# A four-stage transformer kernel on eight cores: a different spread of background quantize jobs in the MLP stage, and a layer norm whose row sums come from two half-row copies

## What is computed

```python
# layer 0, "attention": linear attention and an inner MLP
a = _ln(num / den, ga, ba)
h = a + (gelu(a @ W1 + b1) @ W2 + b2)          # W1 1024x4096, W2 4096x1024
x = _layernorm(x + (h + x))
# layer 0, feed-forward: FP4 block quantization of activations and weights
x = _layernorm(x + fp4_linear(silu(fp4_linear(x, w_gate)) * fp4_linear(x, w_up), w_down))
# layer 1, causal softmax attention, then a squared-relu feed-forward
x = _layernorm(x + attention(x))
x = _layernorm(x + ffn(x))

def fp4_quant_dequant(x):      # blocks of 16 along the last dim
    scale = max(|xb|) / 6
    q = GRID[searchsorted(MID, |xb / scale|)] * sign(xb) * scale
```

## Time and profile before

| what | us |
|---|---|
| median of the two runs | 6672.61 |
| the two runs | 6623.13 and 6722.09 |
| time of the profiled execution | 6682.19 |
| its span (slowest core, core 3) | 6679.5 |
| spans of the eight cores | 6587.1 to 6679.5 |
| DVE busy in the span | 3081.2 (46%) |
| PE busy in the span | 3082.8 (46%) |
| ACT busy in the span | 1331.5 (20%) |
| MLP of phase 1, from the first job at its head to the last job after it | 1613 to 3025 |

### The profile page before, as it was taken

The page is one execution under the profiler, slowest core; times in us unless marked ns, Lnnn a source line. Parts: engine busy times, 40 slices in busy tenths (PEclk is TensorE's granted clock), DMA queues, the critical chain, the costliest instruction groups (busy, mean ns, idle before and its releaser), DMA issues.

```text
span 6679.5 us, 50329 instructions; the slowest of 8 cores (6587.1 to 6679.5 us)
## 1 busy us (share of the span) xinstructions
PE 3082.8 (46%) x11857; PEld 1206.4 (18%) x11857; DVE 3081.2 (46%) x6040; ACT 1331.5 (20%) x2575; POOL 166.1 (2%) x315
## 2 busy tenths in 40 slices
PE   5436154000515243430355555542876666667553
PEld 2112012000202021210123222211321111112321
DVE  4453635642262625348782838473433333333442
ACT  3213110300101011110112111112023333333223
POOL 0000000011000000000000000000000000000000
PEclk8657565555757676665577777776865555557676
DMA  3111010037221212120000000000200000000201
GB/s 49 32 29 21 29 24 14 25 60 158 72 71 60 83 55 89 38 95 5 19 1 29 1 29 1 20 0 21 43 13 1 0 0 0 0 0 24 40 1 51
DMA packets 101208, 217.43 MB, mean 33 GB/s; under 512 B 13506, under 2 KB 17858, under 8 KB 99906
## 3 DMA queue, kind: packets, MB, share of 16 engines
q0 software_dynamic: 39008, 102.27, 7.2%
q1 hardware_dynamic: 61922, 111.96, 5.0%
HBM read 226.26 MB, written 38.27 MB: 40 GB/s over the span
## 4 chain that ended last, share of the span: by engine, by line
DVE 36%; PE 31%; issue 13%; DMA 9%; ACT 8%; DVEq 2%; POOL 1%; SPq 1%; ACTq 0%; POOLq 0%
PE ps L350 17%; DVE QSC L921 8%; PE ps L1127 4%; PE ps L1106 3%; DVE xstage L1138 3%; PE ps L804 2%; DVE QG L872 2%; PE psb L383 2%; ACT ROT L1113 2%; DVE QSC L895 2%; DVE QSC L897 2%; ACT DUM L847 1%; DVE QSC L912 1%; DVE QSC L914 1%; DVE QSC L923 1%
## 5 line engine op out<-in xcount | busy, mean ns | idle before, releaser
L350 PE MATMUL ps<-G 128*128 128x512 f16 (+1 forms) x3328 | 816.1, 409 | 1057.4 <-ACT G L785 600.8
L350 PEld LDWEIGHTS ps<-G 128*128 128x128 f16 x3328 | 362.8, 111 | 1486.0 <-issue 1251.2
L921 DVE TENSOR_TENSOR QSC<-QSC 128x1024 f16<-128x1024 f16 (+2 forms) x888 | 544.1, 613 | 93.4 <-DVE QSC L895 0.9
L350 PE MATMUL ps<-WAbB,G 128*128 128x512 f16 x1536 | 411.1, 429 | 211.0 <-DMA BR<-bq_row 115.2
L1113 ACT ACTIVATE ROT<-ps 128x512 f16<-128x512 f32 x640 | 375.2, 597 | 635.3 <-DVE G L1148 305.7
L1127 PE MATMUL ps<-ROT,GV 128*65 128x512 f16 x640 | 398.3, 622 | 154.4 <-DVE ROT L1120 110.0
L804 PE MATMUL ps<-WAbB,G 128*128 128x512 f16 x1024 | 299.5, 463 | 263.8 <-DMA WAbB<-w2scr 195.0
L888 ACT ACTIVATE xstage<-xstage 128x1024 f32<-128x1024 f32 (+1 forms) x68 | 70.1, 1031 | 1540.5 <-DVE bct L881 892.6
L1106 PE MATMUL ps<-G 64*128 64x512 f16 x640 | 374.7, 606 | 0.0
L383 PE MATMUL psb<-identb_s,G 128*128 128x128 f16 x640 | 82.1, 304 | 597.6 <-DVE G L394 446.9
L1120 DVE TENSOR_TENSOR ROT<-ROT,trimask_s 128x128 f16<-128x128 f16 x256 | 57.7, 226 | 490.0 <-ACT ROT L1113 469.3
(11 more groups left out here) (189 smaller groups left out, 4049.2 us busy)
## 6 DMA issues: line engine op xcount, KB each, us to landing
WAbB<-w2scr SPq DMA_DIRECT2D x256, 256.0 KB, 4.7
xstage<-w_gate POOLq DMA_DIRECT2D x22, 512.0 KB, 4.4
xstage<-w_up POOLq DMA_DIRECT2D x22, 512.0 KB, 4.4
WAbB<-wgoA SPq DMA_DIRECT2D x44, 256.0 KB, 4.0
ROT<-x POOLq DMA_DIRECT2D x32, 256.0 KB, 4.0
WAbB<-W POOLq DMA_DIRECT2D x32, 256.0 KB, 8.9
w2scr<-WAbB SPq DMA_DIRECT2D x32, 256.0 KB, 8.7
xstage<-w_down POOLq DMA_DIRECT2D x16, 512.0 KB, 4.4
```

Source lines behind the costliest of these rows:

```text
L350: last = h.matmul(psbanks[i], lhs_list[j], rhs_list[j][i], start=(j == 0), stop=(j == nchain - 1 and not extra))
L921: lambda h: h.tensor_tensor(Q, Q, C, op=ALU.add))
```

## The change

Two edits. In the MLP of phase 1 the drain at the head of a chunk takes six jobs where it took four, and the two drains after the half-chunks take two where they took three. The number of jobs in a chunk stays ten, and their order is the same.

In `ln_plain_tile` the in-place 1024-wide Copy becomes two 512-wide Copies into `DUM`, so there are four ACT instructions of one size. `ln_stats_math` loses its `full_sum` form: the two sums are added first (one more tiny DVE instruction). The tile is no longer written back by ACT.

```diff
-        def ln_stats_math(slot, full_sum=False):
+        def ln_stats_math(slot):
-            if full_sum:
-                p.op("vector", [sk(0)], [sk(4)],
-                     lambda h, b0=b0: h.tensor_scalar(STAT[:, b0 + 4:b0 + 5],
-                                                      STAT[:, b0:b0 + 1],
-                                                      1.0 / D, None, op0=ALU.mult))
-            else:
...
+            p.op("vector", [sk(0), sk(1)], [sk(4)],
+                 lambda h, b0=b0: h.tensor_tensor(STAT[:, b0 + 4:b0 + 5], STAT[:, b0:b0 + 1],
+                                                  STAT[:, b0 + 1:b0 + 2], op=ALU.add))
+            p.op("vector", [sk(4)], [sk(4)],
+                 lambda h, b0=b0: h.tensor_scalar(STAT[:, b0 + 4:b0 + 5], STAT[:, b0 + 4:b0 + 5],
+                                                  1.0 / D, None, op0=ALU.mult))
...
             for tc in range(TC):
-                bg_drain(4)
+                bg_drain(6)
...
                         ln_plain_tile(ROT, sl, R, tt)
-                    bg_drain(3)
+                    bg_drain(2)
...
-            p.op("scalar", [src.k(sblk)], [src.k(sblk), sk(0)],
-                 lambda h, b0=b0: h.activation(src.blk(sblk), src.blk(sblk), AF.Copy,
-                                               accum_out=STAT[:, b0:b0 + 1]))
-            for i_, c0 in ((2, 0), (3, 512)):
+            for i_, (c0, func) in enumerate(((0, AF.Copy), (512, AF.Copy),
+                                             (0, AF.Square), (512, AF.Square))):
                 p.op("scalar", [src.k(sblk)], [sk(i_), "DUMk"],
-                     lambda h, c0=c0, i_=i_, b0=b0: h.activation(
-                         DUM[:, :], src.blk(sblk, c0, c0 + 512), AF.Square,
+                     lambda h, c0=c0, func=func, i_=i_, b0=b0: h.activation(
+                         DUM[:, :], src.blk(sblk, c0, c0 + 512), func,
                          accum_out=STAT[:, b0 + i_:b0 + i_ + 1]))
-            mAP, rAP, mk_, rk_ = ln_stats_math(slot, full_sum=True)
+            mAP, rAP, mk_, rk_ = ln_stats_math(slot)
```

## The result

The changed kernel is slower by 1.48%: ratio 1.0148, 95% interval 1.0093 to 1.0203, which just leaves open whether it is over 2%. Its median is 6780.15 us (11 runs), that of the kernel before 6718.3 (10 runs). The profiled execution took 6720.52 us, with a span of 6717.9.

The account below looks back on a forecast made before the run. The prediction took hand-overs to bound the kernel, chiefly PE idle 600.8 us before Gelus held behind quantize jobs. Jobs 94.0, earlier adds -9.3 and norm +21.3 gave +106.0 on 6682.19: 6788 us, range 6735 to 6835 (forecast's own 6745 to 6825).

Parts of the forecast that it names:

- The jobs' term: Phase 1's MLP: four full-width quantize jobs move from PE's cover to the path, 23.5 us each, +94.0 us.
- the narrow ones cancel: Covered jobs in phase 1's MLP: narrow jobs 52 and 64 before, 55 and 64 after, so four full-width jobs move.
- The give-back: Second half-chunks of phase 1's MLP: shorter cover lets the residual add start earlier, by 2.7, 5.8, 0.8 and 0: -9.3 us.
- The norm's term: Layer norm: ACT's fourth instruction adds 0.38 us a tile, exposed in 56 of 64 tiles, +21.3 us.
- The test I had named for this term: Norm term is wrong if DVE's last-Square wait stays at 1.48 us a tile while tiles keep their pace.
- The half-spread of 50 us: Whole kernel: the two runs shown lie 99 us apart, so a run can miss the sum by some 50 us.
- The free norm: Rival, layer norm: ACT's extra instruction costs 0 to 0.09 us on the path, 6767 to 6772 us; chance 0.08.
- the uncovered third job: Rival, MLP half-chunks: third job was never covered, so shedding it repays the head, 6703.5 us; chance 0.05.
- this rival: Rival, MLP up stages: three lose clock to the last one's rate, 3 x 10.5 = 31 us, 6820 us; chance 0.12.
- Cheaper jobs at the head: Rival, first head of the MLP: longer run hides loads, 17.9 us a job, 6766 us; chance 0.03.

## Why the prediction was right

**The mechanism.** Each step of the argument from the earlier trace rows is in the changed profile: the absolute value ahead of the Gelus, the eight jobs in a row, the 20 us of idle DVE under the half-chunk (20.71), the stand of 178 us (forecast near 180), the sum of 709.8 (near 710).

**The jobs' term, +94.0.** The first head grew by 47.1 us and the end shrank by 23.6, as two periods and one. That the 47.1 is so near is in part luck, since the head starts up to 28 us apart on the four cores; but from the first job of the head to the first Gelu it is 75.7 to 77.4 us on the eight cores before and 122.1 to 123.4 after, two periods of 23.2. The three runs grew by 56.7. Counting their jobs one by one gives 23.5 (a full one more), 20 (the added one is narrow) and 24, since of a run's last job only the part up to its absolute value counts. That is 67.5, and the prediction had 70.5: "the narrow ones cancel" was 3 us off.

**The give-back, -9.3.** This term was sized on one core, and it differs from core to core: over the four chunks the second half-chunk's add had started later than the 0.2 us behind PE by 12.7, 12.5, 13.7 and 7.9 us in sum on cores 4 to 7, all with a clock of 0.653 or 0.654. On core 6 it was 4.9, 3.7, 3.4 and 1.7 us. After the change it is 0.2 us behind PE's end in every chunk on every core, as predicted. With the median of the first three chunks on die 1, 11.1, the runs come to 67.5 - 11.1 + 6 x 0.38 = 58.7, against 56.7 measured.

**The norm's term, +21.3.** 3.33 us a tile, to the hundredth; 5.6 and 5.8 us in the two stretches of 15 tiles, where 5.7 was expected; phase 4's tail 5.1. The estimate worked out from the figures of the Trainium skill's page "ScalarE: Activation LUTs", section "What ACT_TABLE_LOAD costs" (5 us for 56 tiles), is ruled out by these stretches. The test I had named for this term was badly put: it went by DVE's wait for the last Square, which I took to grow, and it fell by 18.0 us. The two waits of the norm were 90.8 + 94.8 us before (the former on L403) and are 115.8 + 76.8 now, 7.0 more, and 64 extra adds at 0.27 us from start to start are 17 more. Together that is the 24 us that 64 tiles at 0.38 give. An idle time shrinks when new work moves into it, and says nothing of the path by itself; the time from first to last does.

**The sum and the range.** +106 forecast; +103.1 on die 1 from equal clocks. The predicted 6788 us was built on an execution with less clock on one die. So it lies high against the profiled execution after (6720.52), and that it lies within 8 us of the median of all (6780.15) is luck: what clock the dies are granted moves that median by more than 8 us. The half-spread of 50 us in the range was for this, but the range doesn't follow from its own description: 6745 is the sum with all lower bounds (72 - 9.3 + 0) and no spread, and 6825 is less than 6788 + 50. It was a judgement.

**The rivals.** The free norm is ruled out by the stretches, the uncovered third job by the drains of 2, 4 and 4 and of 6, 3 and 1. The change cost the up stages no clock: in its profiled execution the four stages took 55.0 to 56.5 us on all eight cores, at a granted clock of 0.94 to 0.97. The last stage of core 3 before, on which this rival was priced (0.79), has its like only on core 2, with 61.3 us. In the execution with the drains alone, two cores, 4 and 5, did take 56.5 to 63.3 us for them, at 0.83 to 0.94, and the other six, with the same drains, 55.0 to 56.6; so that loss doesn't go with the drains. Cheaper jobs at the head: the run of eight shows the same 5.6 us of load before each.

## What to carry to other kernels

Count background jobs by what covers them, not by how evenly they are spread: the price of a move is the number of jobs that leave the cover times their full period. A job delays another engine through the one instruction that it puts into that engine's list, so that instruction belongs behind the work that PE waits for, and not earlier than it is due. Before filling a cover further, compare DVE's sum with PE's over the same stretch, and before moving a load ahead, look for the last instruction that is declared to use its buffer.

## What was not expected of the hardware

That a lower granted clock lengthens some stages and not others: in one execution of the kernel before, phase 4's tail took 275.7 to 276.3 us on six cores at 0.75 or 0.76 and 297 us on cores 0 and 1 at 0.67, while the 15 tiles at the end of phase 2 took 90.6 us on all eight. And that a time of ACT's can be predicted from instructions alone: a further 512-wide summing instruction cost 0.79 to 0.83 us a tile (11.9 and 12.5 us in 15 tiles), near the sum of its 629 ns and the 186 ns of the read that follows it.
